# A fused Griffin-block and MLP kernel on one core: u transposed by VectorE's blocks and sixteen DMAs, and the mixer's x and y products at other places

## The chip, the cores and the metric

The kernel runs on one NeuronCore of a Trainium2 chip. The metric is the time of one execution on the device in microseconds. Engines by their short names: PE is TensorE, DVE is VectorE, ACT is ScalarE, POOL is GpSimd, SP is the queue that mostly issues the DMAs. Each engine runs its own list of instructions in order, and lists meet only in semaphores.

## What is computed

The input is x, 4 x 1024 x 256 in float32; the output has the same shape. Two layers, each followed by a LayerNorm over the last dimension without scale or shift:

```
t   = rmsnorm(x, norm1_w)
xb  = causal_conv4(t @ Wx) + conv_b
a, b from sigmoid(xb @ Wa), sigmoid(xb @ Wi), lam      h = scan(a * h + b)
h1  = x + (h * gelu(t @ Wy)) @ Wo
u   = rmsnorm(h1, norm2_w)
row = layernorm(x + h1 + (gelu(u @ Wg) * (u @ Wu)) @ Wd)            D = 256, H = 1024
out = layernorm(row + relu(row @ W1 + b1) @ W2 + b2)
```

## The kernel before, in words

**Tiles.** The 4096 tokens are cut into 8 chunks of 512 tokens; two chunks make a sequence. An activation has its tokens on the partitions (four tiles of 128 tokens x 256) or, behind a T in its name, its features (two tiles of 128 x 512 tokens). The matmuls want features on the partitions, so t, u and the first layer's row (x1) are transposed once per chunk. Each fp32 matmul is split in three: an operand is kept as hi (rounded to fp32r) and lo (the rest), and a product is hi*hi + hi*lo + lo*hi. `product` (L458) makes one 128 x 512 output in 6 matmuls of 512 columns; `product_by_tokens` (L463) uses 256 columns.

**Periods and rounds.** After a prologue and a first period, `round_of(r)` runs for r = 8 to 63 on every engine; r = 8p + m, with m the round in period p. In period p three chunks are worked on at a time:

- the gated MLP of chunk p: unit m, that is `gate(r)`, `up(r)` and `down(r - 1)` on PE, gelu on ACT (`gelu_gate`), the product gate times up on DVE (`gate_times_up`), hi on POOL (`gate_hi`), lo on DVE (`gate_lo`);
- the mixer of chunk n = p + 1, spread over the period: x product (m = 0), convolution (m = 0 to 2), `mix_decay` and `mix_input` (m = 3), y product (m = 4), scan and `mix_out` (m = 5), h1 and u (m = 6 and 7);
- the second layer (units w = r - 11 of chunks p - 1 and p - 2): `mlp_up(w)`, `relu(w)` on ACT, `hidden_lo(w)` on DVE, `mlp_down(w - 1)`.

**The order of the work** is written out by hand in the five `round_of`s; there is no planner. What each is behind matters for this case:

- PE, round of m = 4 (L795 on): `gate`, `up`, `down(r - 1)`, `mlp_up`, `mlp_down(w - 1)`, `mix_y`. At m = 7: `gate`, `up`, eight transposes of u (`transpose_u`, L610, in `transposed`, L469), `down`, `mlp_up`, `mlp_down`. At m = 0: the same, with `mix_x` last.
- ACT, m = 4 (L1172 on): `gelu_gate`, `exp_decay`, `square_decay`, `relu(w)` (L1080; waits for `mlp_up(w)` of the same round), `gate_scale` (the square roots, L1018, with a table load before them), another table load. m = 5: `gelu_gate`, `gelu_y`, `hy_hi`, `relu`. m = 6: `square_h1`, `gelu_gate`, `relu`. m = 7: `gelu_gate`, `split_hi` of u from PSUM, `relu`.
- DVE, m = 4 (L1623 on): `second_sum`, `gate_times_up`, `gated_input`, `gate_lo`, `room`, `statistics`, `hidden_lo`. m = 5: `scan_both` (waits for `gate_scale`), `gate_times_up`, `gated`, `hy_lo` (L1453), `gate_lo`, `hidden_lo`. m = 6: `add_mix`, `transpose_blocks` of t, `gate_times_up`, `gate_lo`, `normalise`, `hidden_lo`.
- POOL, m = 5: `gate_hi`, `norm_t` of chunk n + 1. m = 6: `gate_hi`, then `norm_u(n)`. m = 7: `gate_hi`, `add_x_h1`.
- SP (L421 on), per chunk: load x, `move_x1`, `move_t`, `store_out`.

**Transposing by blocks.** From chunk 3 on t, and for six chunks x1, don't go through PE: DVE's `transpose` turns each 32 x 32 block in place into `t_blocks` (L1301), and sixteen DMAs of 32 KB from SP (`move_blocks`, L383) carry the blocks across partitions, 32 partitions x 2 pieces of 512 B each. Tokens then stand in another order, which `in_order` and `by_token` (L219 on) put right in the next access pattern. u of all chunks is transposed by PE into the two PSUM banks MIX and MIX + 1, which the mixer's products use too.

`uT_hi` and `uT_lo` exist once: they may be written after `up` of the last unit of the chunk before. `mix_out` begins with this wait:

```
            def mix_out(c, bank=MIX, qs=range(PAIRS)):
                pe.wait_ge(hy_lo_ready, 2 * (c - 1) + 2)
```

Of the kernel before, what the change touches and what calls it, by code (L numbers as in the profile page):

```python
# [28 lines left out]
def griffin_mlp_kernel(nc, x, norm1_w, Wx, Wy, conv_w, conv_b, Wi, Wa, lam, Wo, norm2_w, Wg, Wu, Wd,  # L29
# [14 lines left out]
    with ctx:  # L44
# [21 lines left out]
        tT_lo = sb("tT_lo", [P, KD, T], FP32R)  # L66
        mT_hi = sb("mT_hi", [P, KD, T], FP32R)
# [157 lines left out]

        MOVES = GROUPS * GROUPS * DMA
# [81 lines left out]
        u_ready = sem("u_ready")  # L308
        first_u_ready = sem("first_u_ready")
# [50 lines left out]
        def _(sync):  # L360
# [22 lines left out]
            def move_blocks(src, dst, moved):  # L383

                blocks = src.rearrange("p (k j a) -> p k j a", k=KD, j=GROUPS)
                placed = dst.rearrange("p (k i a) -> p k i a", k=KD, i=GROUPS)
                for i in range(GROUPS):
                    for j in range(GROUPS):  # L390
                        rows_in = slice(i * BLOCK, (i + 1) * BLOCK)
                        rows_out = slice(j * BLOCK, (j + 1) * BLOCK)
                        sync.dma_start(placed[rows_out, :, i, :], blocks[rows_in, :, j, :]).then_inc(moved, DMA)

            def move_t(c):
                sync.wait_ge(t_blocks_ready, KD * (c - BLOCKWISE + 1))
                move_blocks(flat(t_blocks), flat(t_raw), t_blocks_moved)

            def move_x1(c):
                sync.wait_ge(x1_blocks_ready, KD * c)  # L400
                move_blocks(flat(normed), flat(gy), x1_blocks_moved)
# [49 lines left out]
        def _(pe):  # L451
# [125 lines left out]
            def mix_x(c, ms=range(KD)):  # L577
                pe.wait_ge(tT_lo_ready, 2 * (c - 2) + 2)
                for m in ms:
                    if c == 2:  # L580
                        pe.wait_ge(h1_ready, 2 * (c - 1) + m + 1)
                    product(psum[MIX + m][:, :], "x", m, tT_hi, tT_lo).then_inc(wx_done, 1)
# [37 lines left out]
            def gate(r):  # L620
                c, m = divmod(r, KH)
                if m == 0:
                    pe.wait_ge(uT_lo_ready, 2 * c + 2)
# [10 lines left out]
                product(gate_bank(r)[:, :], "g", m, uT_hi, uT_lo).then_inc(gate_done, 1)  # L634
# [160 lines left out]
            def round_of(r):  # L795
# [3 lines left out]
                if units(r):  # L799
# [76 lines left out]
        def _(act):  # L876
# [77 lines left out]

            def split_x1_hi(c):
# [117 lines left out]
            def gelu_gate(r):  # L1073
# [3 lines left out]
                nc.scalar.activation(gu_raw[:, r % SLOTS, :], gate_bank(r)[:, :],  # L1077
# [94 lines left out]
            def round_of(r):  # L1172
# [3 lines left out]
                if mixing and m == 1:  # L1176
# [117 lines left out]
        def _(dve):  # L1294
# [13 lines left out]

            def transpose_x1_blocks(c):

                dve.wait_ge(uT_done, 2 * (c + 2))
# [199 lines left out]
            def gate_times_up(r):  # L1511
                dve.wait_ge(gelu_ready, r + 1)
                dve.wait_ge(up_done, r + 1)
                nc.vector.tensor_tensor(gu_raw[:, r % SLOTS, :], up_bank(r)[:, :], gu_raw[:, r % SLOTS, :],  # L1514
                                        ALU.mult).then_inc(gu_ready, 1)
# [107 lines left out]
            def round_of(r):  # L1623
# [22 lines left out]
                if m == 6 and p >= 2 and n + 1 < CHUNKS:  # L1646
                    transpose_blocks(n + 1)
                if units(r):
                    gate_times_up(r)
                if mixing:  # L1650
                    if m == 0 and p >= 2:
# [15 lines left out]
                    if m == 7 and p >= 2:  # L1667
                        split_lo(uT_lo, uT_hi, uT_hi_ready, uT_lo_ready, n)
# [4 lines left out]
                if m == 6 and second:  # L1673
# [141 lines left out]
        def _(pool):  # L1815
# [46 lines left out]
            def norm_u(c):  # L1862
                rms(h1_squares(c), ss2, h1_squared, rms2_ms, rstd2, rms2_rstd)
                pool.wait_ge(uT_done, 2 * c)
# [41 lines left out]
            def round_of(r):  # L1906
# [16 lines left out]
                if p == 1 and m == 7:  # L1923
# [6 lines left out]
                if m == 4 and second:  # L1930
# [4 lines left out]
                if mixing:  # L1935
                    if m == 6 and p >= 2:
                        norm_u(n)
                    if n + 1 < CHUNKS:
                        if m == 2:
                            rms(x_squares(n + 1), ss1, x_squared, rms1_ms, rstd1, rms1_rstd)  # L1940
                        if m == 5:
# [64 lines left out]
```

## Time and profile before

| | |
|---|---|
| median of 3 runs | 587.22 us (586.84 to 587.23) |
| the profiled execution | 587.02 us, of which 585.2 us span |
| PE, DVE, ACT, POOL busy | 578.5, 401.0, 314.6, 203.8 us |
| one period of 8 rounds | 70.0 us |
| mean granted clock of PE | 0.998 of full |

The span goes from the first to the last instruction on the engines; 1.8 us lie around it. Matmuls overlap in the pipeline, so the duration of one (390 ns for 512 columns) is longer than the distance from start to start (0.23 us), and a row of the chain gives the distance.

### The profile page before, as it was taken

The page shows a single profiled execution, that of the slowest core. Times are in us where ns is not written, and L with a number is a line of the kernel's source. Part 1 is how long each engine was busy: PE and PEld are TensorE (multiplying, and loading weights), DVE is VectorE, ACT ScalarE, POOL GpSimd, SP SyncE. Part 2 cuts the span into 40 slices and gives each one's busy share as a digit, 9 for nine tenths or more (in the row PEclk, how much of TensorE's full clock was granted, in tenths as well). Part 3 has the DMA queues.
Part 4 walks back from the last instruction along what each step waited for, and adds up shares of the span by engine and source line. Part 5 has one row for each costly group of instructions (what it writes and reads, how often), then busy time and mean ns, then how long its engine had stood idle before and what let it go on. Part 6 is the DMA issues. An engine that isn't in the chain of part 4 may idle for free.

```text
span 585.2 us, 9307 instructions
## 1 busy us (share of the span) xinstructions
PE 578.5 (99%) x3441; PEld 511.9 (87%) x3441; DVE 401.0 (69%) x729; ACT 314.6 (54%) x600; POOL 203.8 (35%) x282
## 2 busy tenths in 40 slices
PE   8999999999999999999999999999999999999996
PEld 8768988898888988898888888889888898888996
DVE  5888958867739668495765848568595765563565
ACT  7977675834548444573446634575343843232454
POOL 2111336273233542255233452424523233140130
PEclk9999999999999999999999999999999999999999
DMA  7400210011100121001210031100200010101011
GB/s 275 149 36 25 84 36 2 2 29 44 37 0 1 27 84 36 1 1 38 73 37 0 1 82 38 26 2 8 65 22 16 1 34 5 34 3 37 1 38 36
DMA packets 27197, 21.46 MB, mean 37 GB/s; under 512 B 3448, under 2 KB 26384, under 8 KB 27152
## 3 DMA queue, kind: packets, MB, share of 16 engines
q1 hardware_dynamic: 27152, 20.87, 11.8%
q8 instruction: 27, 0.44, 0.3%
q14 instruction: 18, 0.15, 0.1%
HBM read 10.89 MB, written 4.19 MB: 26 GB/s over the span
## 4 chain that ended last, share of the span: by engine, by line
PE 97%; DVE 1%; POOL 0%; issue 0%; ACT 0%; DVEq 0%; POOLq 0%; ACTq 0%
PE psum L454 18%; PE psum L456 18%; PE psum L455 18%; PE psum L465 11%; PE psum L467 11%; PE psum L466 11%; PE psum L545 2%; PE psum L472 1%; PE psum L838 1%; PE psum L510 1%; PE psum L676 1%; PE psum L678 1%; PE psum L674 1%; PE psum L572 1%; PE psum L529 1%; PE psum L489 0%
## 5 line engine op out<-in xcount | busy, mean ns | idle before, releaser
L1903 POOL TENSOR_SCALAR gu_hi<-gu_raw 128x512 fp32r<-128x512 f32 x64 | 54.4, 851 | 262.0 <-DVE gu_raw L1514 262.0
L1092 ACT ACTIVATE hid_raw<-psum,vecs 128x512 f32<-128x512 f32 x56 | 38.4, 686 | 115.4 <-PE psum L456 115.3
L1514 DVE TENSOR_TENSOR gu_raw<-psum,gu_raw 128x512 f32<-128x512 f32 x64 | 44.0, 687 | 69.9 <-PE psum L456 69.9
L1524 DVE TENSOR_TENSOR hid_lo<-hid_raw,hid_hi 128x512 fp32r<-128x512 f32 x56 | 40.7, 728 | 47.2 <-ACT hid_hi L1096 47.2
L465 PE MATMUL psum<-w_d_hi,gu_hi 128*128 128x256 f32 x256 | 72.2, 282 | 0.0
L465 PE MATMUL psum<-w_hi,hid_hi 128*128 128x256 f32 x256 | 71.9, 281 | 0.2 <-DVE hid_lo L1524 0.2
L467 PE MATMUL psum<-w_d_hi,gu_lo 128*128 128x256 f32 x256 | 71.8, 281 | 0.0
L467 PE MATMUL psum<-w_hi,hid_lo 128*128 128x256 f32 x256 | 71.8, 281 | 0.0
L466 PE MATMUL psum<-w_lo,hid_hi 128*128 128x256 f32 x256 | 71.7, 280 | 0.0
L466 PE MATMUL psum<-w_d_lo,gu_hi 128*128 128x256 f32 x256 | 71.7, 280 | 0.0
L1077 ACT ACTIVATE gu_raw<-psum 128x512 f32<-128x512 f32 x64 | 38.1, 595 | 50.3 <-PE psum L456 49.7
L1519 DVE TENSOR_TENSOR gu_lo<-gu_raw,gu_hi 128x512 fp32r<-128x512 f32 x64 | 50.2, 784 | 19.2 <-POOL gu_hi L1903 19.2
L465 PEld LDWEIGHTS psum<-w_d_hi,gu_hi 128*128 128x128 f32 x256 | 48.1, 188 | 3.1 <-DVE gu_lo L1519 0.7
L465 PEld LDWEIGHTS psum<-w_hi,hid_hi 128*128 128x128 f32 x256 | 48.2, 188 | 2.7 <-DVE hid_lo L1524 0.6
L454 PE MATMUL psum<-uT_hi,w_g_hi 128*128 128x512 f32 x128 | 50.4, 394 | 0.0
L454 PE MATMUL psum<-uT_hi,w_u_hi 128*128 128x512 f32 x128 | 50.0, 391 | 0.1
L466 PEld LDWEIGHTS psum<-w_d_lo,gu_hi 128*128 128x128 f32 x256 | 48.1, 188 | 2.1
L466 PEld LDWEIGHTS psum<-w_lo,hid_hi 128*128 128x128 f32 x256 | 48.1, 188 | 2.1
L456 PE MATMUL psum<-uT_hi,w_u_lo 128*128 128x512 f32 x128 | 49.9, 390 | 0.0
L455 PE MATMUL psum<-uT_lo,w_g_hi 128*128 128x512 f32 x128 | 49.9, 390 | 0.0
L456 PE MATMUL psum<-uT_hi,w_g_lo 128*128 128x512 f32 x128 | 49.9, 389 | 0.0
L455 PE MATMUL psum<-uT_lo,w_u_hi 128*128 128x512 f32 x128 | 49.8, 389 | 0.0
(237 smaller groups left out, 1530.7 us busy)
## 6 DMA issues: line engine op xcount, KB each, us to landing
out_dram<-row SPq DMA_DIRECT2D x15, 256.0 KB, 2.4
xs<-in_L_attn_x_dram SPq DMA_DIRECT2D x7, 512.0 KB, 3.7
gy<-normed SPq DMA_DIRECT2D x96, 32.0 KB, 1.9
t_raw<-t_blocks SPq DMA_DIRECT2D x80, 32.0 KB, 1.9
raw_gud<-in_L_attn_Wg_dram SPq DMA_DIRECT2D x1, 1024.0 KB, 8.1
raw_gud<-in_L_attn_Wu_dram SPq DMA_DIRECT2D x1, 1024.0 KB, 10.2
raw_gud<-in_L_attn_Wd_dram SPq DMA_DIRECT2D x1, 1024.0 KB, 12.4
raw_gud<-in_L_ffn_W_dram SPq DMA_DIRECT2D x1, 1024.0 KB, 6.6
```

What stands on the lines that cost most here:

```text
L454: nc.tensor.matmul(dst, w_hi[n][:, k, cols], hi[:, k, :], start=(k == 0), stop=False)
L455: nc.tensor.matmul(dst, w_hi[n][:, k, cols], lo[:, k, :], start=False, stop=False)
L456: return nc.tensor.matmul(dst, w_lo[n][:, k, cols], hi[:, k, :], start=False, stop=(k == KD - 1))
L465: nc.tensor.matmul(dst, hi, w_hi[n][:, k, :], start=start, stop=False, skip_group_check=True)
L466: nc.tensor.matmul(dst, hi, w_lo[n][:, k, :], start=False, stop=False, skip_group_check=True)
L467: return nc.tensor.matmul(dst, lo, w_hi[n][:, k, :], start=False, stop=stop, skip_group_check=True)
L1077: nc.scalar.activation(gu_raw[:, r % SLOTS, :], gate_bank(r)[:, :], ACT.Gelu_apprx_tanh).then_inc(gelu_ready, 1)
L1092: nc.scalar.activation(raw, hidden, ACT.Relu, bias=vec("b1", m)).then_inc(relu_ready, 1)
L1514: nc.vector.tensor_tensor(gu_raw[:, r % SLOTS, :], up_bank(r)[:, :], gu_raw[:, r % SLOTS, :], ALU.mult).then_inc(gu_ready, 1)
L1519: nc.vector.tensor_tensor(gu_lo[:, r % SLOTS, :], gu_raw[:, r % SLOTS, :], gu_hi[:, r % SLOTS, :].bitcast(FP32), ALU.subtract).then_inc(gu ...
L1524: nc.vector.tensor_tensor(hid_lo[:, w % SLOTS, :], hid_raw[:, w % SLOTS, :], hid_hi[:, w % SLOTS, :].bitcast(FP32), ALU.subtract).then_inc ...
L1903: nc.gpsimd.tensor_scalar(gu_hi[:, r % SLOTS, :], gu_raw[:, r % SLOTS, :], 1.0, 0.0, ALU.mult, ALU.add).then_inc(gu_hi_ready, 1)
```

## The change

For chunks 3 to 7, u is turned by DVE into `u_blocks` and carried by sixteen DMAs into `u_raw`: eight from SP (i = 0, 1), four from ACT before and four after `gelu_gate` of round m = 7. ACT then makes `uT_hi` and DVE `uT_lo` from `u_raw`, behind `relu` and `hidden_lo` of that round. `u_blocks` and `u_raw` lie over `mT_hi` and `mT_lo`. The first gate of a chunk waits for the first half of uT_lo, and for the second before its second step. In these chunks gelu and the product of gate and up put the tokens back in order. Moved from period 2 on: the x product of chunk n + 1 to the end of round m = 7 (chunk 3's stays in round 16), with the split of its tT in m = 6; the y product within m = 4 ahead of `down`; `norm_t` and the block transposes of t to m = 4; `norm_u` ahead of `gate_hi` in m = 6; the second LayerNorm's statistics to m = 6, its normalisation to m = 7; both convolution starts into m = 0.

```diff
+        with nc.sbuf_tensor("u_blocks", [P, KD, T], FP32) as u_blocks, nc.sbuf_tensor("u_raw", [P, KD, T], FP32) as u_raw:
+            pass
         mT_hi = sb("mT_hi", [P, KD, T], FP32R)
...
+            def move_u(c):
+                sync.wait_ge(u_blocks_ready, KD * (c - BLOCKWISE + 1))
+                move_blocks(sync, flat(u_blocks), flat(u_raw), u_blocks_moved, (0, 1))
...
                 if c >= 4:
+                    move_u(c - 1)
                     store_out(c - 4)
             for c in range(CHUNKS - 4, LAST - 1):
                 move_x1(c + 1)
+                if c + 3 < CHUNKS:
+                    move_u(c + 3)
                 store_out(c)
# PE
...
                 if m == 0:
-                    pe.wait_ge(uT_lo_ready, 2 * c + 2)
+                    pe.wait_ge(uT_lo_ready, 2 * c + (1 if c >= BLOCKWISE else 2))
...
-                product(gate_bank(r)[:, :], "g", m, uT_hi, uT_lo).then_inc(gate_done, 1)
+                for k in range(KD):
+                    if m == 0 and k == KD - 1:
+                        pe.wait_ge(uT_lo_ready, 2 * c + 2)
+                    last = product_step(gate_bank(r)[:, :], "g", m, k, uT_hi, uT_lo)
+                last.then_inc(gate_done, 1)
...
                     up(r)
+                if mixing and m == 4 and p >= 2:
+                    mix_y(n)
                 if mixing and m == 3 and p >= 1:
                     mix_decay(n)
-                if mixing and m == 7 and p >= 2:
-                    transpose_u(n)
                 if units(r - 1) and r != KH:
                     down(r - 1)
...
-                if mixing and m == 0 and p >= 2:
+                if r == 2 * KH:
                     mix_x(n)
-                if mixing and m == 4 and p >= 1:
+                if m == 7 and p >= 2 and n + 1 < CHUNKS:
+                    mix_x(n + 1)
+                if r == KH + 4:
                     mix_y(n)
# ACT
...
+            def move_u(c, i):
+                act.wait_ge(u_blocks_ready, KD * (c - BLOCKWISE + 1))
+                move_blocks(act, flat(u_blocks), flat(u_raw), u_blocks_moved, (i,))
+
+            def split_u_hi(c):
+                act.wait_ge(up_done, KH * c)
+                act.wait_ge(u_blocks_moved, MOVES * (c - BLOCKWISE + 1))
+                for f in range(KD):
+                    nc.scalar.activation(uT_hi[:, f, :], u_raw[:, f, :], ACT.Copy).then_inc(uT_hi_ready, 1)
...
+                if mixing and m == 7 and p >= 2:
+                    move_u(n, 2)
                 if units(r):
                     gelu_gate(r)
                 if mixing:
-                    if m == 0 and p >= 2:
+                    if m == 7 and p >= 2:
+                        move_u(n, 3)
+                    if m == 6 and p >= 2 and n + 1 < CHUNKS:
+                        split_t_hi(n + 1)
+                    if r == 2 * KH:
                         split_t_hi(n)
...
-                if mixing:
-                    if m == 7 and p >= 2:
-                        split_hi(uT_hi, uT_done, uT_hi_ready, n)
                 for w in second_units(r):
                     relu(w)
...
                     if m == 0:
                         conv_start(n, 0)
+                        if p >= 3:
+                            conv_start(n, 1)
+                    if m == 7 and p >= 2:
+                        split_u_hi(n)
                     if m == 4:
                         gate_scale(n)
# DVE
...
-                if m == 6 and p >= 2 and n + 1 < CHUNKS:
-                    transpose_blocks(n + 1)
+                if m == 6 and second:
+                    statistics(s, 1, 0, s2_ready)
+                    statistics(s, 1, 1, s2_ready)
                 if units(r):
                     gate_times_up(r)
+                if m == 6 and p >= 2 and n + 1 < CHUNKS:
+                    split_t_lo(n + 1)
+                if m == 6 and mixing and p >= 2:
+                    transpose_u_blocks(n)
...
-                    if m == 7 and p >= 2:
-                        split_lo(uT_lo, uT_hi, uT_hi_ready, uT_lo_ready, n)
                 if units(r):
                     gate_lo(r)
...
-                if m == 6 and second:
+                if m == 7 and second:
                     normalise(s, 1, 0, out_ready)
...
-                if m == 4 and second:
-                    statistics(s, 1, 0, s2_ready)
-                    statistics(s, 1, 1, s2_ready)
...
                 for w in second_units(r):
                     hidden_lo(w)
+                    if m == 4 and p >= 2 and n + 1 < CHUNKS:
+                        transpose_blocks(n + 1)
+                    if m == 7 and mixing and p >= 2:
+                        split_u_lo(n)
# POOL
...
-                if p == 1 and m == 7:
+                if mixing and m == (7 if p == 1 else 6):
                     norm_u(n)
                 if r < UNITS:
                     gate_hi(r)
...
+                if m == 4 and p >= 2 and n + 1 < CHUNKS:
+                    norm_t(n + 1)
+                if m == 6 and second:
                     for q in range(PAIRS):
                         ln_scale(s, 1, q)
```

## Rows read from the trace of the kernel before

**Rows 1.** The page: the span, and TensorE's busy time, share and instructions.

```profile
span 585.2 us, 9307 instructions
...
PE 578.5 (99%) x3441; PEld 511.9 (87%) x3441; DVE 401.0 (69%) x729; ACT 314.6 (54%) x600; POOL 203.8 (35%) x282
```

**Rows 2.** The list of waits of TensorE: us in total, times, longest.

```profile
PE psum L465 <- DVE hid_lo L1524: 0.2, 1, 0.2
```

**Rows 3.** The chain that ended last: start, length; one set of transposes of u.

```profile
204.18 0.87 PE psum L472 x8
```

**Rows 4.** TensorE's timeline, rounds 20 and 21: start, duration of one.

```profile
180.10 0.39 PE L456 MATMUL psum<-x1T_hi,w_lo 128*128 128x512 f32 x1
...
181.74 0.40 PE L454 MATMUL psum<-tT_hi,w_y_hi 128*128 128x512 f32 x1
...
184.47 0.39 PE L454 MATMUL psum<-uT_hi,w_g_hi 128*128 128x512 f32 x1
...
191.38 0.38 PE L465 MATMUL psum<-w_o_hi,mT_hi 128*128 128x256 f32 x1
```

**Rows 5.** ScalarE's timeline, round 20.

```profile
180.77 0.67 ACT L1092 ACTIVATE hid_raw<-psum,vecs 128x512 f32<-128x512 f32 x1
...
182.03 1.28 ACT L1021 ACT_TABLE_LOAD   x1
183.32 1.15 ACT L1021 ACTIVATE xv<-xv 128x512 f32<-128x512 f32 x2
```

**Rows 6.** VectorE's timeline, round 21.

```profile
183.98 1.29 DVE L1434 TENSOR_TENSOR inp<-inp,xv 128x512 f32<-128x512 f32 x2 [0.27 <-ACT xv L1021]
...
188.21 0.68 DVE L1450 TENSOR_TENSOR gy<-gy,xv 128x512 f32<-128x512 f32 x1
...
188.87 1.04 DVE L1450 TENSOR_TENSOR gy<-gy,xv 128x512 f32<-128x512 f32 x1
189.83 1.49 DVE L1456 TENSOR_TENSOR mT_lo<-gy,mT_hi 128x512 fp32r<-128x512 f32 x2
```

**Rows 7.** The timeline of VectorE and TensorE at chunk 7's `mix_out`.

```profile
470.16 1.47 DVE L1456 TENSOR_TENSOR mT_lo<-gy,mT_hi 128x512 fp32r<-128x512 f32 x2
...
471.71 0.36 PE L465 MATMUL psum<-w_o_hi,mT_hi 128*128 128x256 f32 x1
```

**Rows 8.** SP's DMA issues: its timeline, then line 393 (ns, minimum, median, maximum).

```profile
2.13 0.24 SPq L407 DMA_DIRECT2D vec_rows<-in_L_attn_conv_b_dram  x1
...
196.47 10.23 SPq L393 DMA_DIRECT2D t_raw<-t_blocks  x16
...
L393 SPq DMA_DIRECT2D t_raw<-t_blocks x80: 585/597/1378, 122.3 to 417.1; - x80
...
DMA to landing us min/median/max: 1.8/1.9/3.0
```

**Rows 9.** Timelines of rounds 21 to 23, and line 1305 (the block transposes).

```profile
189.35 4.17 POOL L1842 TENSOR_SCALAR t_raw<-xs,rstd 128x256 f32<-128x256 f32 x4
...
198.84 0.70 POOL L1828 TENSOR_SCALAR rstd<-ss 128x4 f32<-128x4 f32 x1
...
201.02 2.29 POOL L1870 TENSOR_SCALAR normed<-h,rstd 128x256 f32<-128x256 f32 x4 [0.20 <-POOL rstd L1831]
...
196.09 0.58 ACT L1077 ACTIVATE gu_raw<-psum 128x512 f32<-128x512 f32 x1
...
202.85 0.60 ACT L1077 ACTIVATE gu_raw<-psum 128x512 f32<-128x512 f32 x1 [1.51 <-PE psum L456]
...
207.46 0.39 PE L456 MATMUL psum<-x1T_hi,w_lo 128*128 128x512 f32 x1
...
207.89 0.69 ACT L1092 ACTIVATE hid_raw<-psum,vecs 128x512 f32<-128x512 f32 x1 [2.15 <-PE psum L456]
...
L1305 DVE STREAM_TRANSPOSE t_blocks<-t_raw x10: 664/684/702, 121.0 to 406.0; 128x512 f32<-128x512 f32 x10
```

**Rows 10.** The chain: TensorE's first matmuls.

```profile
1.51 3.78 PE psum L838 x16
```

More of the change, by code:

```diff
@@ L224, in by_token, with move_blocks @@
             return ap.rearrange("p (t i s) -> p t i s", i=GROUPS, t=TT)
+        def move_blocks(queue, src, dst, moved, groups=range(GROUPS)):
+            blocks = src.rearrange("p (k j a) -> p k j a", k=KD, j=GROUPS)
+            placed = dst.rearrange("p (k i a) -> p k i a", k=KD, i=GROUPS)
+            for i in groups:
+                for j in range(GROUPS):
+                    rows_in = slice(i * BLOCK, (i + 1) * BLOCK)
+                    rows_out = slice(j * BLOCK, (j + 1) * BLOCK)
+                    queue.dma_start(placed[rows_out, :, i, :], blocks[rows_in, :, j, :]).then_inc(moved, DMA)
         MOVES = GROUPS * GROUPS * DMA
@@ L308, in griffin_mlp_kernel @@
         u_ready = sem("u_ready")
+        u_blocks_ready = sem("u_blocks_ready")
+        u_blocks_moved = sem("u_blocks_moved")
         first_u_ready = sem("first_u_ready")
@@ L381, in store_out @@
                                    rows[c % 2][:, 2 * q:2 * q + 2, :]).then_inc(out_stored[c % 2], DMA)
[L383 to L393, printed above, removed]
             def move_t(c):
                 sync.wait_ge(t_blocks_ready, KD * (c - BLOCKWISE + 1))
-                move_blocks(flat(t_blocks), flat(t_raw), t_blocks_moved)
+                move_blocks(sync, flat(t_blocks), flat(t_raw), t_blocks_moved)
             def move_x1(c):
                 sync.wait_ge(x1_blocks_ready, KD * c)
-                move_blocks(flat(normed), flat(gy), x1_blocks_moved)
+                move_blocks(sync, flat(normed), flat(gy), x1_blocks_moved)
+            def move_u(c):
+                sync.wait_ge(u_blocks_ready, KD * (c - BLOCKWISE + 1))
+                move_blocks(sync, flat(u_blocks), flat(u_raw), u_blocks_moved, (0, 1))
             for q in range(PAIRS):
@@ L1076, in gelu_gate @@
                     act.wait_ge(gu_lo_ready, r - SLOTS + 1)
-                nc.scalar.activation(gu_raw[:, r % SLOTS, :], gate_bank(r)[:, :],
+                dst, gate = gu_raw[:, r % SLOTS, :], gate_bank(r)[:, :]
+                if r >= KH * BLOCKWISE:
+                    dst, gate = by_token(dst), in_order(gate)
+                nc.scalar.activation(dst, gate,
                                      ACT.Gelu_apprx_tanh).then_inc(gelu_ready, 1)
@@ L1175, in round_of @@
                 mixing = n < CHUNKS
-                if mixing and m == 1:
+                if r == 2 * KH + 1 or r == KH + 1:
                     conv_start(n, 1)
@@ L1307, in transpose_blocks, with transpose_u_blocks, split_u_lo @@
                                         ).then_inc(t_blocks_ready, 1)
+            def transpose_u_blocks(c):
+                dve.wait_ge(u_ready, u_tiles(c))
+                for k in range(KD):
+                    nc.vector.transpose(u_blocks[:, k, :].rearrange("p (j t s) -> p t j s", j=GROUPS, t=TT),
+                                        normed[:, :, k * P:(k + 1) * P].rearrange("p t (j s) -> p t j s", j=GROUPS)
+                                        ).then_inc(u_blocks_ready, 1)
+            def split_u_lo(c):
+                for f in range(KD):
+                    dve.wait_ge(uT_hi_ready, 2 * c + f + 1)
+                    nc.vector.tensor_tensor(uT_lo[:, f, :], u_raw[:, f, :], uT_hi[:, f, :].bitcast(FP32),
+                                            ALU.subtract).then_inc(uT_lo_ready, 1)
             def transpose_x1_blocks(c):
-                dve.wait_ge(uT_done, 2 * (c + 2))
+                if c + 1 < BLOCKWISE:
+                    dve.wait_ge(uT_done, 2 * (c + 2))
+                else:
+                    dve.wait_ge(u_blocks_ready, KD * (c + 2 - BLOCKWISE))
                 dve.wait_ge(x1_ready, TT * c + TT)
@@ L1513, in gate_times_up @@
                 dve.wait_ge(up_done, r + 1)
[L1514 to L1515 removed]
+                gu, up = gu_raw[:, r % SLOTS, :], up_bank(r)[:, :]
+                if r >= KH * BLOCKWISE:
+                    gu, up = by_token(gu), in_order(up)
+                nc.vector.tensor_tensor(gu, up, gu, ALU.mult).then_inc(gu_ready, 1)
             def gate_lo(r):
@@ L1863, in norm_u @@
                 rms(h1_squares(c), ss2, h1_squared, rms2_ms, rstd2, rms2_rstd)
-                pool.wait_ge(uT_done, 2 * c)
+                if c <= BLOCKWISE:
+                    pool.wait_ge(uT_done, 2 * c)
+                else:
+                    pool.wait_ge(u_blocks_ready, KD * (c - BLOCKWISE))
                 if by_blocks(c - 2):
@@ L1935, in round_of @@
                 if mixing:
-                    if m == 6 and p >= 2:
-                        norm_u(n)
                     if n + 1 < CHUNKS:
```

7 lines of the change are left out of this document (3 added, 4 removed).

## The prediction, made before the changed kernel was built or run

> **What bounds the kernel now.** I read the page's busy shares first: TensorE is busy for 578.5 of 585.2 us, and no other engine over 70% [rows 1]. Then the list of waits: once the periods run, TensorE has waited a single time, for 0.2 us [rows 2]. So the time is the length of TensorE's instruction list, and two things can change it: fewer columns through TensorE, or a new wait of TensorE. Last I read the timelines of one period (chunk 3's mixer, chunk 2's units: rounds 16 to 23, of which 20 to 23 matter), to see which operand TensorE takes just in time. The reader should see one place there. The output product of the mixer (`mix_out`) starts at 191.38 [rows 4]; the last `hy_lo`, without which it may not start, ends at 189.83 + 1.49 = 191.32 [rows 6]. The slack is 0.06 us. Chunk 7 shows the same: 470.16 + 1.47 = 471.63 against 471.71 [rows 7]; chunks 4, 5 and 6 repeat it, so there are five such places in the stretch that the change touches. That no wait is listed there doesn't mean room.
>
> **Removed from TensorE.** Eight 128x128 transposes of u per chunk, for chunks 3 to 7. One set takes 0.87 us of TensorE's list [rows 3], and there are five: -4.35 us. The products, 512 or 256 columns each, stay as many as they were.
>
> **The y product moves ahead within round 4 (m = 4).** It is 12 matmuls, 181.74 to 184.47, 2.73 us [rows 4]. Now it runs right after `up`, ahead of `down`, `mlp_up` and `mlp_down`. For TensorE alone that is a change of order at no cost, but ScalarE's list isn't changed: in round 4 it runs square_decay, then `relu(w)`, which waits for `mlp_up(w)`, and only then the table load and the square root of `gate_scale`. Before, the last matmul of `mlp_up` starts at 180.10 [rows 4]. In round 7 such a relu starts at 207.89, 0.43 us after that matmul (207.46) [rows 9]; here ScalarE, busy until then, came at 180.77 [rows 5]. After, that matmul starts at 180.10 + 2.73 = 182.83 and the relu at 183.26: 2.49 us later. The table load (182.03) and the roots (183.32) follow it back to back [rows 5], VectorE's scan input (183.98) had waited for the first root [rows 6], and scans, `gated`, `hy_hi` and `hy_lo` follow without a gap to 191.32. So `hy_lo` ends at 193.81, while TensorE, whose work up to `mix_out` is the same sum in another order, is there at 191.38. New wait: 2.49 - 0.06 = 2.43 us, five times: +12.15 us. A second new wait, of `mlp_up` in round 5 for the gelu behind the late table load (about 0.3 us), lies inside it, as TensorE is early there.
>
> What else stands in that stretch: the t tiles are scaled on POOL in round 4 (four tiles in 4.17 us or less [rows 9], from about 180.4) and transposed by VectorE behind `hidden_lo(w)`, 2 x 0.684 us [rows 9]: hid_hi at 184.50, hidden_lo to 185.2, transposes to 186.5, and the first root is then at 183.98 + 2.49 = 186.47. That just fits, and costs nothing. LayerNorm's statistics leave that place for round 6, where VectorE idles before `gate_times_up`. Bounds of this term: nothing of the 2.49 shed is +12.15; the only stretched operation of the chain is the second product for `gy` (1.04 us against 0.68 unstretched [rows 6]), and if the scaling of t, gone from round 5, was what stretched it, 0.36 is shed, five times: +10.35. Chunk 7 has no such scaling beside it and the operation took 1.04 there too, so I take +12.15.
>
> **u by blocks.** I count in the time of before, so that the wait at `mix_out` drops out. The squares of h1 end at 196.1; POOL's rms and four scalings took from 198.84 to 201.02 + 2.29 = 203.31, 4.47 us, behind gate_hi [rows 9]. Now norm_u comes ahead of gate_hi(6): u at about 200.7. VectorE waits for it and transposes twice 0.684: 202.1. Behind that wait stands gate_lo(6), done at 202.8 or, if POOL is slowed, 203.5; TensorE wants it at 204.18, hence nothing. Each small copy takes SP 10.23 / 16 = 0.64 us to issue and lands 1.9 us after its start [rows 8]. SP issues 8 of them, from 202.1 to 207.2. ScalarE has issued none in this trace: its price is bounded by 0.24 (a 1 KB load) and 1.38 (the longest of such copies) [rows 8]; I take 0.64, the same shape from the other queue. Four go ahead of gelu(7): to 204.7, so that gelu, ready at 202.85 [rows 9], ends at 205.3, and `mlp_up` wants it at 205.6. Four follow it: to 207.9; the last lands at 209.2. relu(12), before at 207.89, now runs from 207.9 to 209.15; split_u_hi ends at 209.8 and 210.3; VectorE's hidden_lo ends at 209.9, and uT_lo is ready at 210.55 and 211.15. TensorE: `down` 1.41 from 204.18, `mlp_up` 1.37, `mlp_down` 1.41, then the x product of the next chunk, 2.73: it wants the two at 211.1 and 211.8. For chunks 3 to 6 that just fits: 0, with 0.5 us to spare. Chunk 7 has no x product of a next chunk behind it, so the gate is wanted at 208.37 and gets its operand at 210.55: +2.2 us. With 0.24 per issue that is 1.75; with 1.38 all five chunks stall, which is the third case below.
>
> The x product itself only moves (its operand by split_t in round 6, whose sixteen copies are issued from 186.5 on, 10 us of SP, inside the first wait), the split convolution start and the permuted gelu have no new instruction: 0. SP has moved t before u and stores the output after it; rows of the output are wanted again only in the next period.
>
> **Sum** against the profiled execution's own 587.02 us: -4.35 + 12.15 + 2.2 = +10.0, 597.0; the median of the runs, 587.22, is 0.2 higher: **597.2**. About 0.2% (1.2 us) is what a measurement of this kernel can tell.
>
> **Rivals.**
> 1. *Clock.* [...] At the start, after idling, 16 matmuls of 128 columns took 3.78 us, 0.236 each [rows 10], against 0.109 in a transpose set [rows 3]; so that stretch lost 1.9 us. After each of the six waits: +11.3, 608.5. Against it: the waits are 2.4 us, short beside the period; nothing in this trace shows a gap of such length amid work. 7%. [...]
> 2. *The queues don't overlap.* If ScalarE's and SP's copies are issued one at a time, all sixteen need 10.2 us from 202.1: gelu(7) is done at 207.8 instead of 205.3 (`mlp_up` waits 2.2), relu at 213.6, the first uT_lo at 214.85 against 211.1: 3.75 for each of chunks 3 to 6 and 6.5 instead of 2.2 for chunk 7, together +19.3, 616.5. [...] 10%. [...]
> 3. *Faster.* The chain from the round-4 relu to `hy_lo` sheds its delay, as POOL no longer works beside it in round 5 and VectorE has lost the statistics. Price: 587.22 - 4.35 + 2.2 = 585.1. It decides only from 2.3 us shed out of 2.49 per chunk (then 5 x 0.17 remain and the total is under -1.2), and the rows give 0.36. 9%, for a misread order more than for the mechanism.
>
> The forecast keeps 74%; its own range is 592.5 to 601. The range given, 592 to 608, reaches to the clock case and leaves out rivals 2 and 3. Faster is rival 3 less 0.01; within 0.2% 0.02; slower the rest.
>
> **What would show it.** Right: no transposes on `normed` after 133 us; TensorE's waits list `mix_out` on `mT_lo`, five times, 2.4 each; ScalarE idle about 2.4 us before the round-4 relu, for TensorE; one wait of chunk 7's gate on uT_lo, 2.2. If the five are near 0 the forecast falls. If the gates of chunks 3 to 6 wait over 3 us each, or issues take 1.2 us while both queues run, rival 2; if matmuls behind a wait are spaced at twice 0.23 us, rival 1.

## The result and the profile after

The changed kernel takes 607.38 us (606.70 to 611.25), before 587.23: ratio 1.0358, 95% interval 1.032 to 1.0397. It is slower, as forecast, but by 20.2 us and not by 10.0. The profiled execution, 611.25 us, is the longest of all (the others took 606.70, 606.92, 607.85 and 608.72), which matters for the clock below.

The page of the changed kernel: span, TensorE's busy time, and the granted clock in 40 slices.

```profile
span 609.5 us, 9326 instructions
...
PE 586.1 (96%) x3401; PEld 515.1 (85%) x3401; DVE 412.9 (68%) x739; ACT 315.2 (52%) x600; POOL 196.7 (32%) x282
...
PEclk9999999999998999989999899999999988999999
```

Forty matmul records are gone (3441 to 3401, the five sets of transposes), yet TensorE is busy for 7.6 us more than in [rows 1]. That can't be work. (The clock's price below comes to 7.6 too; that is chance, since this figure also holds the transposes that are gone and the ends of matmuls in front of waits.) The clock row gives the direction: five slices are at 8, where that of before has 9 throughout the periods. First the waits of TensorE, which answer to [rows 2]: us in total, times, longest.

```profile
PE psum L478 <- DVE mT_lo L1512: 9.0, 5, 1.8
PE psum L467 <- DVE uT_lo L1359: 6.5, 5, 2.9
PE psum L857 <- POOL ident L2016: 1.5, 1, 1.5
PE psum L467 <- ACT gu_raw L1110: 1.2, 6, 0.2
```

Five waits at `mix_out` (9.0), five at the first gate of a chunk (6.5), one in the prologue that the kernel before has too (1.5), and small ones of `mlp_up` for the gelu. ScalarE's timeline of round 20, against [rows 5], has the reason of the first:

```profile
179.85 1.14 ACT L1046 ACTIVATE xv<-decay 128x512 f32<-128x512 f32 x2
183.38 0.69 ACT L1125 ACTIVATE hid_raw<-psum,vecs 128x512 f32<-128x512 f32 x1 [2.39 <-PE psum L469]
...
184.66 1.28 ACT L1051 ACT_TABLE_LOAD   x1
185.95 1.15 ACT L1051 ACTIVATE xv<-xv 128x512 f32<-128x512 f32 x2
```

The relu waits 2.39 us for TensorE and starts at 183.38 against 180.77, 2.61 us later; 0.12 of it is this execution's general lag (its gelu in the same stretch starts at 176.51 against 176.39), so 2.49, as forecast. The table load and the roots follow back to back. At `mix_out` (TensorE's timeline, [rows 4] before):

```profile
191.86 0.28 PE L480 MATMUL psum<-w_hi,hid_lo 128*128 128x256 f32 x1
193.99 0.39 PE L478 MATMUL psum<-w_o_hi,mT_hi 128*128 128x256 f32 x1 [1.85 <-DVE mT_lo L1512]
```

From start to start 2.13 us stand where 0.12 should: 2.0 us lost. Measured this way, over all matmuls from 120 us on, the five places at `mix_out` lose 9.8 us, `mlp_up` 1.7, the gates of chunks 3 to 6 4.3 (1.03 to 1.12 each), chunk 7's gate 3.0. Then the clock: busy time, granted clock and DMA by stretches of 2 us around the first of these waits (PE alone).

```profile
190.00:192.00 2.00, 2.00 (x16) 1.00 0.20 50
192.00:194.00 2.00, 0.15 (x3) 1.00 0.20 49
194.00:196.00 2.00, 2.00 (x10) 0.59 0.20 49
196.00:198.00 2.00, 2.00 (x12) 0.55 0.20 49
198.00:200.00 2.00, 2.00 (x13) 1.00 0.01 4
```

TensorE did next to nothing from 192 to 194; then the granted clock is 0.59 and 0.55 (read by half microseconds it is 0.50 from 194.5 to 197.5), and 17 matmuls of 256 columns come 0.21 apart and not 0.117: 1.6 us. It happened behind four of the five waits at `mix_out`, and behind chunk 7's gate (1.1 us): 7.6 us in this execution. That is five of the ten waits at `mix_out` and the gates; behind the other five it stayed at 1.00.

The first matmul behind each of these waits, and of the small ones of `mlp_up`, is slower by 0.11 us at a granted clock of 1.00 too (0.22 and not 0.117 to the next at 193.99, 0.34 and not 0.23 at 216.35); with what little follows that is about 2 us in all. Sum of the profiled execution: -4.35 + 18.8 of waits + 7.6 of clock + 2.0 of such first matmuls = 24.1, of 611.25 - 587.02 = 24.2.

Why the gates wait, VectorE's and POOL's timelines of round 23:

```profile
211.02 1.76 DVE L1577 TENSOR_TENSOR gu_lo<-gu_raw,gu_hi 128x512 fp32r<-128x512 f32 x1 [0.74 <-POOL gu_hi L1968]
212.71 2.39 DVE L1536 TENSOR_SCALAR row<-row,ln_mv,ln_rstd 128x256 f32<-128x256 f32 x4
215.02 0.68 DVE L1582 TENSOR_TENSOR hid_lo<-hid_raw,hid_hi 128x512 fp32r<-128x512 f32 x1
215.62 1.28 DVE L1359 TENSOR_TENSOR uT_lo<-u_raw,uT_hi 128x512 fp32r<-128x512 f32 x2
```

```profile
210.95 2.98 POOL L1942 TENSOR_TENSOR h<-h,xs 128x512 f32<-128x512 f32 x2
```

```profile
213.30 1.15 ACT L983 ACTIVATE uT_hi<-u_raw 128x512 fp32r<-128x512 f32 x2
```

ScalarE's first uT_hi is there from about 213.9. VectorE starts its part at 215.6, because `gate_lo` took 1.76 us (0.7 alone) and the four normalisations 2.39 (1.38 in round 22 before), both while POOL adds h1 and x. Of the four only the first is longer, 1.42 us against 0.40. The trace of before holds the same pair, later against each other:

```profile
205.65 3.00 POOL L1877 TENSOR_TENSOR h<-h,xs 128x512 f32<-128x512 f32 x2
206.49 1.02 DVE L1519 TENSOR_TENSOR gu_lo<-gu_raw,gu_hi 128x512 fp32r<-128x512 f32 x1
```

`gate_lo` took 1.02 us there. In both traces it ends 0.54 us behind the first of the two additions: 207.50 against 206.96, and 212.78 against 212.24. What the neighbour cost was a little less than what was left of the addition when it started: 0.33 us with 0.47 left, and 1.07 with 1.22 left.

It isn't the DMAs that are late. Their issues, side by side in two queues (ns: minimum, median, maximum):

```profile
L239 SPq DMA_DIRECT2D u_raw<-u_blocks x40: 585/598/1222, 206.0 to 506.5; - x40
L239 ACTq DMA_DIRECT2D u_raw<-u_blocks x40: 592/620/959, 206.0 to 506.9; - x40
```

ScalarE's 0.62 us is SP's 0.60 of [rows 8], and neither doubles while both run: from start to start the first four of each come 0.63 to 0.65 us apart on SP and 0.65 to 0.79 on ScalarE.

### The profile page after: what moved, and what is told of

Same layout as the page of the kernel before. It is cut to its first block, busy times and chain, and to the rows that moved or that the text cites. A ratio compares the mean times of both kernels' runs of the same rounds, so it can differ in the third digit from the quotient of the medians.

```text
span 609.5 us, 9326 instructions
## 1 busy us (share of the span) xinstructions
PE 586.1 (96%) x3401; PEld 515.1 (85%) x3401; DVE 412.9 (68%) x739; ACT 315.2 (52%) x600; POOL 196.7 (32%) x282
## 4 chain that ended last, share of the span: by engine, by line
PE 75%; DVE 10%; issue 5%; POOL 5%; ACT 4%; ACTq 0%; POOLq 0%; DVEq 0%
PE psum L467 14%; PE psum L469 14%; PE psum L468 14%; PE psum L478 9%; PE psum L480 9%; PE psum L479 8%; DVE row L1536 2%; PE psum L558 2%; POOL normed L1935 2%; DVE gu_lo L1577 2%; DVE gy L1506 1%; POOL ln_rstd L1950 1%; DVE xv L1497 1%; ACT L1051 1%; POOL gu_hi L1968 1%
## 5 line engine op out<-in xcount | busy, mean ns | idle before, releaser
L1577 DVE TENSOR_TENSOR gu_lo<-gu_raw,gu_hi 128x512 fp32r<-128x512 f32 x64 | 53.9, 842 | 24.3 <-POOL gu_hi L1968 24.3
L467 PE MATMUL psum<-uT_hi,w_g_hi 128*128 128x512 f32 x128 | 51.8, 405 | 6.6 <-DVE uT_lo L1359 6.5
```

What stands on the lines that cost most here:

```text
L467: nc.tensor.matmul(dst, w_hi[n][:, k, cols], hi[:, k, :], start=(k == 0), stop=False)
L1577: nc.vector.tensor_tensor(gu_lo[:, r % SLOTS, :], gu_raw[:, r % SLOTS, :], gu_hi[:, r % SLOTS, :].bitcast(FP32), ALU.subtract).then_inc(gu ...
```

## The experiments

All are compared with the kernel before on the same chip (587.0 to 587.3 us).

**One move alone.** The kernel before, with nothing of the change but the y product's place.

```diff
                     up(r)
+                if mixing and m == 4 and p >= 2:
+                    mix_y(n)
...
-                if mixing and m == 4 and p >= 1:
+                if r == KH + 4:
                     mix_y(n)
```

> The kernel before with one move: the y product of chunks 3 to 7 right behind up. Theory A (the relu of round 4, late by the y product, holds the square roots and with them hy_lo): five waits of TensorE on mT_lo of 1.7 to 2.1 us, five of about 0.2 us on the gelu of round 21, no wait on uT_lo; lost in waits 10 to 11 us, and up to 1.6 us more at each wait behind which the granted clock falls, so 597 to 605. Rival B (the waits at mix_out come from the new work for u, or from t's block transposes having moved to round 4): none of that is here, so the waits at mix_out are under 0.5 us each and the time is within 2 us of 587.2.

604.05 us, ratio 1.0283 (1.0268 to 1.0299). TensorE's waits:

```profile
PE psum L465 <- DVE mT_lo L1458: 9.0, 5, 1.9
...
PE psum L454 <- ACT gu_raw L1079: 0.9, 5, 0.2
```

The same five waits without any of the work for u. From start to start they and the five of `mlp_up` lose 11.6 us, and three falls of the clock about 4.7: this single line is 17 of the 20 us. The rival that puts the loss into the work for u is out as the main cause.

**The order of ScalarE and VectorE mended.** The changed kernel, with the lists of rounds 4 and 5 put so that the chain to `hy_lo` doesn't hang on the relu:

```diff
                     if m == 4:
                         exp_decay(n)
                         square_decay(n)
+                        if p >= 2:
+                            gate_scale(n)
+                            act.preload_act_table(ACT.Gelu_apprx_tanh)
...
-                    if m == 4:
+                    if m == 4 and p == 1:
                         gate_scale(n)
                         act.preload_act_table(ACT.Gelu_apprx_tanh)
...
-                if m == 5 and mixing:
+                if m == 5 and mixing and p == 1:
                     scan_both(n)
+                if m == 5 and mixing and p >= 2:
+                    gated(n)
+                    hy_lo(n)
...
-                    if m == 5:
+                    if m == 5 and p == 1:
                         gated(n)
-                    if r == FROM or m == 5 and p >= 2:
+                    if r == FROM:
                         hy_lo(n)
...
                     if m == 4:
                         room(n)
+                        if p >= 2:
+                            scan_both(n)
```

> The changed kernel with ScalarE's square roots (and their table loads) ahead of the round-4 relu, and VectorE's scans ahead of that round's hidden_lo, gated and hy_lo ahead of gate_times_up, from period 2 on. Theory A: hy_lo no longer hangs on the relu; TensorE's waits on mT_lo fall from 1.8 to under 0.5 us each, no fall of the clock behind them; 10 us and the clock's share less than the changed kernel, 592 to 597, the gates' waits on uT_lo unchanged (1.0 four times, 3.0). Rival B (mix_out is late by the length of VectorE's own list in rounds 4 and 5): the waits keep over 1 us and the time stays over 602.

600.39 us, ratio 1.0226 (1.0209 to 1.0243): 7.0 less than the changed kernel, not 10 or more. The waits at `mix_out` are gone altogether. But a new one of the same family came:

```profile
PE psum L467 <- DVE uT_lo L1362: 6.6, 5, 2.9
PE psum L467 <- ACT gu_raw L1110: 4.8, 4, 1.5
```

```profile
201.07 1.15 ACT L971 ACTIVATE tT_hi<-t_raw 128x512 fp32r<-128x512 f32 x2 [3.97 <-DMA t_raw<-t_blocks]
```

ScalarE stood 3.97 us before the split of the next chunk's t, whose sixteen copies now land later against the work: SP issues them from 188.48 us on (186.61 in the changed kernel), since the scans now stand ahead of the transposes of t, while the work behind them comes sooner. Behind it VectorE's u transposes, the first four issues, gelu(23) and `mlp_up` are all late. While TensorE still waited at `mix_out`, this was hidden.

**The gates' wait.** Two ways of testing the same reading. First the normalisations of the previous stream, on VectorE's list, go behind the second units' loop, and so behind `split_u_lo`:

```diff
                     gate_lo(r)
-                if m == 7 and second:
-                    normalise(s, 1, 0, out_ready)
-                    normalise(s, 1, 1, out_ready)
...
                         statistics(f, 0, 1, s1_ready)
+                if m == 7 and second:
+                    normalise(s, 1, 0, out_ready)
+                    normalise(s, 1, 1, out_ready)
```

> The changed kernel with the second LayerNorm's normalisation of round m = 7 put behind split_u_lo on VectorE. Theory A (the late gate of chunks 3 to 6 is VectorE's list: gate_lo and the four normalisations run beside POOL's sum of h1 and x and take 1.8 and 2.4 us instead of 0.7 and 1.4): uT_lo comes 2.3 us sooner less what waits then for uT_hi, the gates of chunks 3 to 6 don't wait, chunk 7's waits 1.0 to 2.0 instead of 3.0; 5 to 6 us faster than the changed kernel, 601 to 602.5. Rival B (ScalarE's eight DMA issues and their landing hold the gates): uT_hi was what came late, so the waits stay at 1.0 and 3.0, and the time at 607.

603.14 us, ratio 1.0273 (1.0255 to 1.0292). The waits of chunks 3 to 6 on uT_lo are gone and chunk 7's is 1.7 (2.9). 4.2 us were won where 5 to 6 were expected: a wait of 1.7 us for `hidden_lo` turned up after the last round, where the final sum, which stands ahead of it on VectorE, waits for the store of the row that is now normalised later, and one of 1.0 for the gelu. Then POOL's sum of h1 and x one round later, which leaves VectorE's list alone:

```diff
                 if r < UNITS:
                     gate_hi(r)
+                if m == 0 and p >= 3:
+                    add_x_h1(p)
...
-                    if m == 7:
+                    if m == 7 and p == 1:
                         add_x_h1(n)
```

> The changed kernel with POOL's sum of h1 and x for chunks 3 to 7 one round later (m = 0 of the next period). Theory A (VectorE's gate_lo and normalisation of round 23 are stretched by POOL working beside them): gate_lo(23) takes 0.7 instead of 1.76 us and the four normalisations 1.4 instead of 2.4, the waits on uT_lo fall from 1.0 to 0 and from 2.9 to 1.0 or less, 600 to 603. Rival B (they are long by themselves, or uT_hi is late too): durations or waits as in the changed kernel, 606 to 608.

599.23 us, ratio 1.0208 (1.0194 to 1.0222), 8.2 us less than the changed kernel. VectorE's list is the same as there, only its neighbour is away:

```profile
209.49 0.69 DVE L1577 TENSOR_TENSOR gu_lo<-gu_raw,gu_hi 128x512 fp32r<-128x512 f32 x1 [0.75 <-POOL gu_hi L1968]
210.10 1.38 DVE L1536 TENSOR_SCALAR row<-row,ln_mv,ln_rstd 128x256 f32<-128x256 f32 x4
```

0.69 and 1.38 in place of 1.76 and 2.39, and one wait on uT_lo is left, 1.3 us for chunk 7. The reading holds. The stretch went with the sum, to a `gate_lo` for which TensorE doesn't wait, again to 0.54 us behind the first addition (219.91 against 219.37):

```profile
218.14 1.77 DVE L1577 TENSOR_TENSOR gu_lo<-gu_raw,gu_hi 128x512 fp32r<-128x512 f32 x1 [0.74 <-POOL gu_hi L1968]
```

The gain is above the 6 that the waits give, since the clock fell less often: once in the profiled execution (600.06 us). Two of the other executions took 598.3 and 598.4 us, with a granted clock of 1.00.

**The clock.** The changed kernel with matmuls of no use in the waits, `ident` times `ident` into a bank that is overwritten next: 17 ahead of `mix_out`, 8 ahead of the gates of chunks 3 to 6, 26 ahead of chunk 7's, in the places of the diff below.

> The changed kernel with matmuls of no use in TensorE's waits: 17 of 128 columns ahead of each mix_out, 8 ahead of the first gate of chunks 3 to 6, 26 ahead of chunk 7's, as long as the waits they stand in. Theory A (5 to 6 us of the loss is the granted clock, which falls to half behind the waits): granted clock 1.00 all the way, no stretch in which matmuls are spaced twice as far, the waits' own time unchanged; 601 to 603. Rival B (the matmuls behind a wait are slow for another reason, or the fillers delay more than they cover): the stretches stay and the time is 607 or more.

617.73 us, ratio 1.0522, far from any expectation: the fillers were sized wrongly. An `ident` matmul in fp32 leaves two records, 0.11 us apart, so 17 of them took 3.7 us from the first to `mix_out` where 2.0 were lost before. The granted clock was 1.00 up to the last matmul, but the time said nothing. At half the number:

```diff
             def mix_out(c, bank=MIX, qs=range(PAIRS)):
+                if c >= BLOCKWISE:
+                    pe.wait_ge(gy_ready, 2 * c + 2)
+                    for _ in range(8):
+                        nc.tensor.matmul(psum[bank][:, 0:P], ident[:, :], ident[:, :], start=True, stop=True)
                 pe.wait_ge(hy_lo_ready, 2 * (c - 1) + 2)
...
+                if m == 0 and c >= BLOCKWISE:
+                    pe.wait_ge(gu_ready, r)
+                    for _ in range(13 if c == LAST else 4):
+                        nc.tensor.matmul(gate_bank(r)[:, 0:P], ident[:, :], ident[:, :], start=True, stop=True)
                 if m == 0:
```

> The changed kernel with the fillers at half their number, since one ident matmul is two passes of 0.109 us and the first set was twice as long as the waits: 8 ahead of each mix_out (1.75 us), 4 ahead of the gates of chunks 3 to 6, 13 ahead of chunk 7's. Theory A (what the waits don't explain is the clock, 5 to 6 us): granted clock 1.00, the small waits left add up with the fillers to the 19 us of the waits, and the time is 587.0 - 4.35 + 19.1 = 601.8, 601 to 603. Rival B (matmuls behind a wait are slow for another reason): 606 or more.

604.39 us (604.24 to 605.02), ratio 1.0297 (1.0283 to 1.0311). The same stretches as above:

```profile
192.00:194.00 2.00, 2.00 (x19) 1.00 0.22 53
194.00:196.00 2.00, 1.94 (x16) 1.00 0.20 50
196.00:198.00 2.00, 2.00 (x15) 1.00 0.24 59
```

Clock 1.00 up to the last matmul (below it only in the last 2 us, without matmuls, as in the kernel before), and no stretch of slow matmuls in the whole trace, though `mix_out` starts no sooner (2.13 us from start to start here too). A kernel that does more is 3.0 us faster than the changed one (medians), and 6.9 against its profiled execution. The two kernels differ only in TensorE's idle time at these places: with 1.95 us of matmuls in the wait at 192.15 the clock reads 1.00, without them 0.59 and 0.55. So the clock falls here because TensorE idles. The expected 601.8 was 2.6 short: the filled places and `mlp_up` lose 19.4 us from start to start and not 19.1, and the expectation left out the slower first matmuls behind them, 1.9 us, about as much as in the changed kernel. By the same measure the changed kernel loses 18.8 at these places, so the fillers cost 0.6 themselves (chunk 7's alone 0.3).

**All three together.** Roots first, normalisation late (while there is a mixer), and the split of t behind the relu on ScalarE and behind `hidden_lo` on VectorE in round 6, so that its DMA wait blocks nobody. The roots as in the diff above; beside them:

```diff
-                if m == 6 and p >= 2 and n + 1 < CHUNKS:
-                    split_t_lo(n + 1)
...
-                if m == 7 and second:
+                if m == 7 and second and not mixing:
                     normalise(s, 1, 0, out_ready)
                     normalise(s, 1, 1, out_ready)
...
+                    if m == 6 and p >= 2 and n + 1 < CHUNKS:
+                        split_t_lo(n + 1)
                     if m == 7 and mixing and p >= 2:
                         split_u_lo(n)
...
+                if m == 7 and second and mixing:
+                    normalise(s, 1, 0, out_ready)
+                    normalise(s, 1, 1, out_ready)
...
-                    if m == 6 and p >= 2 and n + 1 < CHUNKS:
-                        split_t_hi(n + 1)
...
+                    if m == 6 and p >= 2 and n + 1 < CHUNKS:
+                        split_t_hi(n + 1)
                     if m == 7 and p >= 2:
                         split_u_hi(n)
```

> Roots and scans first, the normalisation behind split_u_lo, and the split of t behind the relu of round m = 6 on ScalarE and behind hidden_lo on VectorE. Theory A (the list orders are the whole loss): no waits on mT_lo, none over 0.5 us for the gates of chunks 3 to 6, chunk 7's 1.5 to 2.5 with at most one fall of the clock: 587.0 - 4.35 + 2 to 5 = 585 to 588. Rival B (the sixteen DMAs alone cost more than the transposes save): over 590.

586.18 us, ratio 0.9984 (0.9974 to 0.9993): 0.9 us faster than the kernel before, where the transposes alone would give 4.35. One wait of the periods is left beside the 0.2 of [rows 2]:

```profile
PE psum L467 <- DVE uT_lo L1362: 1.7, 1, 1.7
```

With the lists in order, the sixteen DMAs of a chunk don't cost more than the transposes save: the price lay in the order, not in the method.

**Chunk 7 by TensorE.** It alone has no x product ahead of its gate. Its transposes and splits go back to the old way (`units` of chunk 7 take gelu and `up` unpermuted, and the two waits that count the blocks follow):

```diff
+                if m == 7 and n == LAST:
+                    transpose_u(n)
                 if units(r - 1) and r != KH:
...
-                if mixing and m == 7 and p >= 2:
+                if mixing and m == 7 and p >= 2 and n < LAST:
                     move_u(n, 2)
...
+                    if m == 7 and n == LAST:
+                        for f in range(KD):
+                            act.wait_ge(uT_done, 6 + f + 1)
+                            nc.scalar.activation(uT_hi[:, f, :], psum[MIX + f][:, :], ACT.Copy).then_inc(uT_hi_ready, 1)
...
-                if r >= KH * BLOCKWISE:
+                if KH * BLOCKWISE <= r < KH * LAST:
                     gu, up = by_token(gu), in_order(up)
...
-                if m == 6 and mixing and p >= 2:
+                if m == 6 and mixing and p >= 2 and n < LAST:
                     transpose_u_blocks(n)
...
+                if m == 7 and n == LAST:
+                    split_lo(uT_lo, uT_hi, uT_hi_ready, uT_lo_ready, n)
```

> The same, with u of chunk 7, which has no x product to cover it, transposed by TensorE as before. Theory A: four sets of transposes saved, 3.5 us, and no wait over 0.5 us but a few: 583 to 586, faster than the kernel before. Rival B: a wait moves elsewhere (gelu of round 23, hidden_lo) and it is no faster than 586.5.

585.10 us, ratio 0.9967 (0.9954 to 0.9979). No wait is left in the list for the periods, and still 1.5 us are missing to 587.06 - 4 x 0.87 = 583.6. Most of them stand in TensorE's timeline as a gap too short for the list:

```profile
185.57 0.39 PE L467 MATMUL psum<-uT_hi,w_g_lo 128*128 128x512 f32 x1
186.03 0.47 PE L465 MATMUL psum<-uT_hi,w_u_hi 128*128 128x512 f32 x1
```

0.46 us and not 0.23 between gate and `up` of round 21, once per period: five times 0.23 is 1.15 us, and 0.26 more are lost once, ahead of an `mlp_up` at 414.43. `up` waits there for the round-4 relu's hid_hi, which stands behind the table load that stands ahead of it here.

**The table load last.** It stays behind the relu, the roots stay in front.

```diff
                         if p >= 2:
                             gate_scale(n)
-                            act.preload_act_table(ACT.Gelu_apprx_tanh)
...
-                    if m == 4 and p == 1:
-                        gate_scale(n)
+                    if m == 4:
+                        if p == 1:
+                            gate_scale(n)
                         act.preload_act_table(ACT.Gelu_apprx_tanh)
```

> x7_last_by_pe with the gelu table loaded after the relu of round m = 4 and not before it. Theory A (the 1.5 us that x7 lacks to 587.06 - 3.5 are five times 0.3 us in which up of round m = 5 waits for that relu's hid_hi, late by the 1.28 us table load): those five gaps go, 583.2 to 584.2. Rival B (the 1.5 us are spread over other gaps): 584.8 or more.

583.36 us (583.03 to 583.49), ratio 0.9927 (0.9914 to 0.9941), on a chip where the kernel before takes 587.3. The expected 583.2 to 584.2 held, and no gap of this kind is left in the periods. This version beats both kernels: four sets of transposes are 3.5 us, and 3.9 were won.

**One queue.** The same, with all sixteen copies of u from SP (both `move_u` calls of ScalarE are gone).

```diff
-            move_blocks(sync, flat(u_blocks), flat(u_raw), u_blocks_moved, (0, 1))
+            move_blocks(sync, flat(u_blocks), flat(u_raw), u_blocks_moved)
```

> The same with all sixteen copies of u issued by SP and none by ScalarE. Theory A (the two queues issue side by side, 0.70 us each while both run, so that one queue alone needs 10.3 us in place of about 6.5): the last copy lands about 3 to 4 us later, the gates of chunks 4 to 6 wait 1 to 3 us for uT_lo, no gate of chunk 3 to 6 sooner; 586 to 594. Rival B (the issues of two queues exclude each other): no later landing, and within 1 us of x9_table_last.

601.67 us, ratio 1.0259 (1.0223 to 1.0296), more than expected. The expectation should have said chunks 3 to 6: the gates of all four wait.

```profile
PE psum L465 <- DVE uT_lo L1362: 12.3, 4, 3.4
```

```profile
201.26 10.62 SPq L239 DMA_DIRECT2D u_raw<-u_blocks  x16
```

```profile
213.23 1.15 ACT L983 ACTIVATE uT_hi<-u_raw 128x512 fp32r<-128x512 f32 x2 [4.71 <-DMA u_raw<-u_blocks]
```

uT_hi starts at 213.2 against 208.5 with two queues, 4.7 us later, more than the 3 to 4 expected; 2.97 to 3.53 us of it show at each gate from start to start. In the profiled execution, 606.81 us and the longest of four, the clock falls behind every one of them, 1.5 to 2.6 us each; the others took 600.68 to 602.06 at a higher mean clock (0.991 against 0.98). ScalarE's queue is worth 18 us here. That also speaks against the rival on the queues by its own measure: if the issues excluded each other, moving them would have cost next to nothing.

## Why the prediction was half right

- *Transposes removed, -4.35.* Right: four sets gave 3.5 us and a little more in the last versions.
- *The y product holds the relu, the relu the roots, the roots hy_lo: +12.15.* Right in every link, and shown by the move alone. It measured 9.8 at `mix_out` and 1.7 at `mlp_up`, 11.5 together. The second lies inside the first, as forecast: the two share the 2.43 of a chunk.
- *The gates of chunks 3 to 6: "that just fits: 0, with 0.5 us to spare".* This step failed: +4.3. The sum followed ScalarE's issues and the landing with care and took VectorE's `hidden_lo` as free at 209.9. In front of it stood `gate_lo` and, moved there by the change, the normalisation, both beside POOL's sum of h1 and x, and the forecast names neither. At their undisturbed durations they would have been done before the relu, and the 0.5 us to spare would have been about right (an estimate from the rows of round 23: its first half at 214.65, wanted at 216.35 - 1.12 = 215.23). They grew by 2.1 us. Moving the sum away shows it. The rows were there: `gate_lo` took 1.02 us beside the same sum in the trace of before, and the gy product of 1.04 [rows 6] was a second case. The forecast asked whether the scaling of t had stretched it; with the scaling gone it still took 1.04 (from 191.51 on), and in both traces it ends 0.54 to 0.55 us behind POOL's `gate_hi`.
- *Chunk 7's gate, +2.2.* The mechanism was right; it measured 3.0. With the stretch moved away it lost 1.4, so the forecast was 0.8 too high without the stretch and 0.8 too low with it.
- *The clock, a rival at 7% with all six falls.* Sized wrong in kind: it isn't a case for itself but a price on each wait, paid behind some. With fillers the median is 3.0 us lower, and in the profiled execution five falls cost 7.6; the forecast's sum had none. The three executions of 606.70 to 607.85 us have a mean granted clock of 0.993, against 0.984 in the profiled one; an estimate from its five falls gives them about two, 3.2 us. The price of one fall, 1.6 us, was near the 1.9 worked out from [rows 10]; the trace of before shows no granted clock below 1.00 in that stretch, so that those 1.9 us were the clock is the forecast's estimate and was not shown.
- *The queues, 10%.* Refuted: 0.62 and 0.60 us side by side, where one at a time would have shown 1.2.
- *Faster, 9%.* Nothing of the 2.49 us was shed. The roots come 2.5 us late, `mix_out` 2.0 and `mlp_up` 0.3.
- *The sum.* +10.0 against +20.2. Of the missing 10.2: 4.3 are the gates of chunks 3 to 6, 0.8 chunk 7's, 3.0 the clock, about 2 first matmuls behind waits, which the forecast left out, less 0.65 for the term of `mix_out`; 0.7 stay open. The fillers have a price of their own (0.6, above), so the clock's share may be 3.6, which would close most of it; no run separates these. That the range's upper end held the median is luck: it reached out to the clock's case, in which six falls were the whole rest, and not to late gates.

## What to carry to other kernels

A bound engine with no idle time can still be just in time for an operand (here by 0.06 us at `mix_out`); a product put ahead of others on it is free only if nothing that it delays stands, in another engine's list, in front of the chain to that operand. So for each moved block, follow what waits for the blocks it overtakes, and what stands behind those waiters in order. Where a change moves instructions next to another engine's, take the durations from rows in which both run (here 1.02 and 1.76 us for a `gate_lo` of 0.69), and ask how much of the other's instruction is left when the moved one starts. Add to each new wait of TensorE the chance of a stretch at a lower granted clock; here it came behind five of ten, at 0.50 for over 3 us, and cost 1.1 to 1.6 us.

## What the runs showed of the hardware

- The granted clock fell to 0.50 behind waits of 1.7 to 1.9 us at `mix_out` in some cases and not in others, in the same kernel and trace (all counts are of the profiled executions): four of five in the changed kernel, three of five with the y product alone, two of five and one of five in the two tests on the gates. It fell behind chunk 7's 2.9 us here and behind all four waits of 2.8 to 3.4 with one queue; behind waits of 0.9 to 1.5 us none was seen, nor behind chunk 7's 1.7. A fall costs about 1.6 us (1.1 at chunk 7's gate, up to 2.6 with one queue). So the time of a kernel with such waits spreads more: 606.7 to 611.25, against 586.84 to 587.66 before.
- VectorE's 128x512 subtraction with both operands in SBUF took 0.69 us alone, 1.02 when POOL's addition of 128x512 tiles had run for 0.84 us and 1.76 when it had run for 0.07; each time it ended 0.54 us behind that addition. A subtraction with one operand in PSUM (`uT_lo<-psum,uT_hi`, before, 205.89) took 0.68 beside the same addition. Four scalings of 128x256 took 2.39 beside it and 1.38 without; only the first was longer, 1.42 against 0.40. So the same instruction of VectorE had three durations here, by POOL's work beside it and by its start against that.
- ScalarE issued a 32 KB copy of 64 pieces in 0.62 us (median of 40); an activation ahead of the next issues overlapped them (changed kernel: gelu at 208.96 for 0.60 us, the next four issues from 208.98 for 2.96), so the issues cost its list 0.58 us less than their sum there.
